# Cross attention over 8192 keys: maxima of the scores from the keys' high parts on two row groups, single score banks, denominators shared out anew

## The reference, cut to what matters

```python
s = q_h @ k_h.T * scale          # 512 x 8192; layer 0 masks keys by mask[q, key]
p = exp(s - max(s, axis=-1))     # softmax over the keys
out_h = (p @ v_h) / p.sum(axis=-1)
x = x + concat(out_h) @ Wo.T + bo
```

## Time and profile before

| | us |
|---|---|
| median of 3 runs | 4553.37 (4545.86 to 4557.13) |
| the profiled execution, its own time | 4563.42 |
| its span (first to last instruction) | 4561.7 |
| cross attention of layer 0, of the span | about 400 to 1595 |
| cross attention of layer 1, of the span | about 2660 to 3730 |
| TensorE busy in the whole span | 4016.3 (88%) |
| VectorE, ScalarE, GpSimd busy | 3028.8, 2097.2, 2085.6 |

### The profile page before, as it was taken

The page is one execution under the profiler, slowest core; times in us unless marked ns, Lnnn a source line. Parts: engine busy times, 40 slices in busy tenths (PEclk is TensorE's granted clock), DMA queues, the critical chain, the costliest instruction groups (busy, mean ns, idle before and its releaser), DMA issues. The chain is left out here.

```text
span 4561.7 us, 51244 instructions
## 1 busy us (share of the span) xinstructions
PE 4016.3 (88%) x17552; PEld 2239.1 (49%) x17552; DVE 3028.8 (66%) x5006; ACT 2097.2 (46%) x2331; POOL 2085.6 (46%) x1224
## 2 busy tenths in 40 slices
PE   7996999999999866669999869999999969769997
PEld 6883344444444242127777634444444425347775
DVE  3334777777777159954777658787877634477776
ACT  2220354555545424322666516555555621347665
POOL 0001698998989715510000029988898940000000
PEclk9996899999999877988999969999999978789998
DMA  8998566665666410011788748988888850308886
GB/s 304 329 335 276 133 143 142 145 142 139 147 133 146 91 42 9 0 66 43 279 300 302 259 133 205 210 205 199 199 201 191 185 125 1 103 30 308 301 304 230
DMA packets 301553, 802.04 MB, mean 176 GB/s; under 512 B 55793, under 2 KB 89329, under 8 KB 263920
## 3 DMA queue, kind: packets, MB, share of 16 engines
q1 hardware_dynamic: 231312, 560.19, 36.3%
q0 software_dynamic: 61280, 221.80, 23.7%
q10 hardware_dynamic: 8704, 16.78, 1.1%
HBM read 484.23 MB, written 98.37 MB: 128 GB/s over the span
## 5 line engine op out<-in xcount | busy, mean ns | idle before, releaser
L855 POOL TENSOR_TENSOR den_pool<-den_pool,prob 128x1024 f32<-128x1024 f32 x444 | 1162.9, 2619 | 54.1 <-ACT prob L696 35.0
L696 ACT ACTIVATE prob<-psum 128x1024 f32<-128x1024 f32 x752 | 768.4, 1024 | 623.7 <-PE psum L610 599.7
L588 PE MATMUL psum<-k_ring,q_stack 98*128 98x512 f32 x2048 | 905.1, 465 | 120.9 <-DVE row_max L746 43.5
L610 PE MATMUL psum<-q_stack,k_ring 98*128 98x512 f32 x2048 | 870.1, 496 | 2.3 <-ACT prob L696 1.3
L746 DVE CUSTOM_DVE_ANT_0 psum<-psum,mask_q 128x512 f32<-128x512 f32 x1024 | 702.5, 706 | 255.0 <-PE psum L588 253.2
L742 DVE TENSOR_REDUCE row_max<-psum 128x1 f32<-128x512 f32 x1024 | 681.5, 688 | 214.5 <-PE psum L588 210.8
L588 PEld LDWEIGHTS psum<-k_ring,q_stack 98*128 98x128 f32 x2048 | 402.6, 197 | 808.9 <-issue 473.0
L1811 DVE TENSOR_TENSOR weight_lo<-weight_raw,weight_hi 128x2048 fp32r<-128x2048 f32 x240 | 547.1, 2289 | 163.0 <-ACT weight_hi L1754 162.8
L1754 ACT ACTIVATE weight_hi<-weight_raw 128x2048 fp32r<-128x2048 f32 x240 | 454.3, 1915 | 42.3 <-DMA weight_raw<-in_L_ffn_w 23.1
L855 POOL TENSOR_TENSOR den_pool<-den_pool,xnT 128x1024 f32<-128x1024 f32 x164 | 419.8, 2560 | 20.4 <-ACT xnT L696 11.3
L610 PEld LDWEIGHTS psum<-q_stack,k_ring 98*128 98x128 f32 x2048 | 405.3, 199 | 45.4 <-ACT prob L696 16.0
(11 more groups left out here) (415 smaller groups left out, 6277.5 us busy)
## 6 DMA issues: line engine op xcount, KB each, us to landing
den_dma<-prob POOLq DMA_DIRECT2D x260, 512.0 KB, 5.2
weight_raw<-in_L_ffn_w SPq DMA_DIRECT2D x120, 1024.0 KB, 6.7
k_ring<-k_hi SPq DMA_DIRECT2D x1024, 64.0 KB, 2.5
weight_raw<-in_L_ffn_Wu SPq DMA_DIRECT2D x60, 1024.0 KB, 7.0
weight_raw<-in_L_ffn_Wd SPq DMA_DIRECT2D x60, 1024.0 KB, 4.9
den_dma<-xnT POOLq DMA_DIRECT2D x92, 512.0 KB, 5.1
k_ring<-k_lo SPq DMA_DIRECT2D x512, 64.0 KB, 3.0
den_pool<-den_dma POOLq DMA_DIRECT2D x48, 512.0 KB, 5.4
```

What stands on the lines that cost most here:

```text
L588: e.matmul(k.bank(maxbank[i % 2]), q_stack[h % n_q][:, i * P:(i + 1) * P], k_ring[:, n % kring, :], start=True, stop=True).then_inc(s_max, 1)
L610: ins = e.matmul(k.bank(kt), k_ring[:, n % kring, kt * P:(kt + 1) * P], q_stack[h % n_q][:], start=not masked, stop=True)
L696: e.activation(prob[g % n_p], k.psum[:, 2 * j2:2 * j2 + 2, :], ACT.Exp, scale=scale).then_inc(s_exp, 1)
L855: e.tensor_tensor(den[:], den[:], tile, ALU.add).then_inc(s_dpool, 1)
```

## The change

- **Maxima from the high parts.** The maximum matmuls use 32 rows, q high against k high. Two matmuls make one step: rows 0 to 31 with one chunk of keys, rows 32 to 63 with the next chunk (both groups of rows of `k_ring` hold the high part; `q_stack` now gets the high part three times, and its low part is loaded by `load_q_lo` after the maxima of the head are through). A step fills two banks (2 and 3, or 4 and 5), and VectorE reduces 1024 columns at once. A head has 32 steps, one for each pair. The step stands between the scores of the pair's two blocks. The maxima run LEAD = 3 steps beyond one head ahead, `top_of_rows` moves from pair 30 to pair 28. The rows of the maximum need not be zero during the maxima, so `zero_rows` is gone.
- **Single score banks.** A block's score fills bank 0 or bank 1, and ScalarE takes exponentials of 512 columns, 64 a head.
- **Denominators.** Layer 0: VectorE adds tiles 0 to 4 (four additions of 128 x 1024 at pairs 3 to 6), GpSimd 18, DMA 9 as before. Layer 1: TensorE sums 11 tiles (pairs 0, 3, ..., 30): a wave has three blocks of values and a fourth matmul of 32 columns of ones, in the fourth column group, so a head has 22 waves; DMA takes 7 tiles with one accumulator and one merge, GpSimd 14 (13 additions).
- **Division in pieces.** The reciprocal and the product of four heads are cut into four pieces of 128 columns each, at pairs 16 to 23.
- Buffers: `prob` has 7 tiles in layer 0 (6 before), `k_ring` 22 and 36 chunks (20 and 32 before), the values come in quarters, and the output weights have a place of their own.

```diff
-LEAD = 1
+LEAD = 3
...
+class Waves:
+
+
+    def __init__(self, by_pe):
+        self.cols = 3 if by_pe else 4
+        self.count = -(-KT // self.cols)
+        self.by_pe = by_pe
+
+    def blocks(self, w):
+        return range(self.cols * w, min(self.cols * (w + 1), KT))
+
+    def sum_block(self, w):
+
+        return 6 * (w // 2) + w % 2
...
+    def step(self, w):
+
+        return -(-(self.cols * (w + 1)) // 2)
...
-    n_q, n_p = 3, 6 if masked else 10
-    kring = NKC + LEAD + (3 if masked else 15)
+    n_q, n_p = 3, 7 if masked else 10
+    kring = 22 if masked else 36
+    if masked:
+        sums = Sums([0, 1, 2, 3, 4], [], list(range(5, PAIRS - 2, 3)))
+    else:
+        sums = Sums([], list(range(0, PAIRS, 3)), [7, 10, 14, 17, 20, 25, 28])
+    waves = Waves(sums.by_pe)
...
-    sums = Sums(range(5, PAIRS - 2, 3), 1) if masked else Sums(range(5, PAIRS - 2, 2), 2)
...
+        return k.psum[:, 2 + 2 * (q % 2):4 + 2 * (q % 2), :].rearrange("p b n -> p (b n)")
...
-                for g, part in enumerate((0, 1, 0)):
-                    e.dma_start(q_stack[h % n_q][g * DH:(g + 1) * DH, :].bitcast(F32), q_hi_lo[part][rows, :]
+                    e.wait_ge(s_score, KT * (h - n_q + 1))
+                for g in range(3):
+                    e.dma_start(q_stack[h % n_q][g * DH:(g + 1) * DH, :].bitcast(F32), q_hi_lo[0][rows, :]
                                 ).then_inc(s_q[h % n_q], 16)
+
+            def load_q_lo(h):
+                e.wait_ge(s_max, PAIRS * (h + 1))
+                e.dma_start(q_stack[h % n_q][DH:2 * DH, :].bitcast(F32), q_hi_lo[1][h * DH:(h + 1) * DH, :]
+                            ).then_inc(s_q[h % n_q], 16)
...
+                if c == LAST_SUM // 2 and h + 1 < H:
+                    load_q_lo(h + 1)
...
+            def maxima(q):
+                h, r = divmod(q, PAIRS)
+                c2, i = divmod(r, TT)
+                n = NKC * h + 2 * c2
+                if r == 0:
+                    e.wait_ge(s_q[h % n_q], 64 * (h // n_q) + 48)
                 if i == 0:
-                    if c == 0:
-                        e.wait_ge(s_q[h % n_q], 48 * (h // n_q + 1))
-                    if c == 0 and h >= n_q:
-                        e.wait_ge(s_zero, h - n_q + 1)
-                    if n < kring:
-                        e.wait_ge(s_ring, n_q + n + 1)
                     e.wait_ge(s_k[n % kring], 48 * (n // kring + 1))
-                if 4 * n + i >= 2:
-                    e.wait_ge(s_red, 4 * n + i - 1)
-
-                e.matmul(k.bank(maxbank[i % 2]), q_stack[h % n_q][:, i * P:(i + 1) * P], k_ring[:, n % kring, :],
-                         start=True, stop=True).then_inc(s_max, 1)
+                    e.wait_ge(s_k[(n + 1) % kring], 48 * ((n + 1) // kring + 1))
+                if q >= 2:
+                    e.wait_ge(s_red, q - 1)
+                for a in range(2):
+                    rows = slice(a * DH, (a + 1) * DH)
+                    ins = e.matmul(max_banks(q)[:, a * KC:(a + 1) * KC], q_stack[h % n_q][rows, i * P:(i + 1) * P],
+                                   k_ring[rows, (n + a) % kring, :], start=True, stop=True)
+                ins.then_inc(s_max, 1)
...
-            def scores(g):
-                h, p = divmod(g, PAIRS)
-                n, j2 = divmod(g, 2)
-                if p == 0:
+            def scores(b):
+                h, t = divmod(b, KT)
+                n, kt = divmod(b, 4)
+                if t == 0:
                     e.wait_ge(s_mlo, h + 1)
-                if g >= 2:
-                    e.wait_ge(s_exp, g - 1)
-                for j in range(2):
-                    kt = 2 * j2 + j
-                    if masked:
-                        e.matmul(k.bank(kt), k.ident_big[:], masks[1][:, 2 * p + j, :], start=True, stop=False)
-                    ins = e.matmul(k.bank(kt), k_ring[:, n % kring, kt * P:(kt + 1) * P], q_stack[h % n_q][:],
-                                   start=not masked, stop=True)
-                ins.then_inc(s_score, 1)
+                    e.wait_ge(s_q[h % n_q], 64 * (h // n_q + 1))
+                if b == 0:
+                    e.wait_ge(s_ring, kring)
+                if b >= 2:
+                    e.wait_ge(s_exp, b - 1)
+                if masked:
+                    e.matmul(k.bank(b % 2), k.ident_big[:], masks[1][:, t, :], start=True, stop=False)
+                e.matmul(k.bank(b % 2), k_ring[:, n % kring, kt * P:(kt + 1) * P], q_stack[h % n_q][:],
+                         start=not masked, stop=True).then_inc(s_score, 1)
...
+                if waves.by_pe:
+                    t = waves.sum_block(w)
+                    ins = e.matmul(vbank[3 * DH:4 * DH, :], k.ones[:, 0:DH],
+                                   prob[(PAIRS * h + t // 2) % n_p][:, t % 2, :], start=w == 0,
+                                   stop=w == waves.count - 1, skip_group_check=True)
...
+                scores(2 * g)
+                if g + PAIRS + LEAD < H * PAIRS:
+                    maxima(g + PAIRS + LEAD)
+                scores(2 * g + 1)
+                waves_after(h, p)
...
+            def exponentials(b):
+                e.wait_ge(s_score, b + 1)
+                if b % 2 == 0:
+                    tile_free(b // 2)
+                e.activation(prob[b // 2 % n_p][:, b % 2, :], k.bank(b % 2), ACT.Exp, scale=scale).then_inc(s_exp, 1)
...
-                    e.reduce_max(out, bank, AXIS_X).then_inc(s_red, 1)
+                    e.reduce_max(out, max_banks(q), AXIS_X).then_inc(s_red, 1)
...
-                e.tensor_tensor_reduce(out=bank, in0=bank, in1=masks[0][:, i, chunk_cols(c)], scale=1.0,
+                    e.wait_ge(s_maskq, 4 * c2 + 2 + i // 2 + 1)
+                e.tensor_tensor_reduce(out=max_banks(q), in0=max_banks(q),
+                                       in1=masks[0][:, i, 2 * c2 * KC:2 * (c2 + 1) * KC], scale=1.0,
...
-            def zero_rows(h):
-                e.wait_ge(s_score, reused_stack(h))
-                e.memset(q_stack[h % n_q][rows_m, :].bitcast(F32), 0.0).then_inc(s_zero, 1)
+            def add_tile(h, j):
+
+                p = sums.by_dve[j + 1]
+                den, tile = den_pool[h % 2], prob[(PAIRS * h + p) % n_p]
+                e.wait_ge(s_exp, 2 * (PAIRS * h + p) + 2)
+                if j == 0:
+                    if h >= 2:
+                        e.wait_ge(s_head, h - 1)
+                    e.tensor_tensor(den[:], prob[PAIRS * h % n_p], tile, ALU.add).then_inc(s_ddve, 1)
+                else:
+                    e.wait_ge(s_ddve, sums.dve_adds * h + j)
+                    e.tensor_tensor(den[:], den[:], tile, ALU.add).then_inc(s_ddve, 1)
...
+            def divide(g, n, cols):
+                e.wait_ge(s_rec, n)
+                e.tensor_tensor(attT[:, g, cols], attT[:, g, cols], den4[:, cols], ALU.mult).then_inc(s_rec, 1)
...
+                if p == LAST_SUM and h + 1 < H:
                     top_of_rows(h + 1)
...
+                if 3 <= p < 3 + sums.dve_adds:
+                    add_tile(h, p - 3)
...
+                if 16 <= p < 24 and h % 4 == 0 and h > 0:
+                    done, cols = 8 * (h // 4 - 1) + p - 16, slice((p - 16) // 2 * P, ((p - 16) // 2 + 1) * P)
+                    (divide if p % 2 else reciprocal)(h // 4 - 1, done, cols)
...
-            def merge(h, a):
...
+            def merge(h):
 
                 e.wait_ge(s_dpool, sums.pool_adds * (h + 1))
-                e.wait_ge(s_ddma[a], 16 * sums.acc_adds[a] * (h + 1))
-                if a > 0:
-                    e.wait_ge(s_merge, 16 * (sums.n_acc * h + a))
-                e.dma_start(den_pool[h % 2][:], den_dma[a][:], accum_op=ALU.add).then_inc(s_merge, 16)
+                e.wait_ge(s_ddma, 16 * len(sums.by_dma) * (h + 1))
+                e.dma_start(den_pool[h % 2][:], den_dma[:], accum_op=ALU.add).then_inc(s_merge, 16)
```

330 lines of the change are left out of this document (168 added, 162 removed).

## The result

The changed kernel takes 5249.65 us (median of 4 runs, 5240.10 to 5263.05) against 4555.25 (4545.86 to 4566.56) before: ratio 1.1525, 95% interval 1.1486 to 1.1564, slower by 15%. That is far outside my range of 4350 to 4710.

A forecast was written before the change was run, and what follows sets the result against it. TensorE bounds layer 0; TensorE and VectorE hold each other up in layer 1. Layer 0 +17 - 18 = -1, layer 1 +74 + 4 - 20 = +58, together +57: 4620 profiled, 4610 median; range 4350 to 4710 (8 in 10).

The forecast's parts named there:

- the clock at 0.97 or above: Expected TensorE clock; its rival, chance 0.06: gaps at steps put a tenth of both stages at 1.2 GHz, 4810 us.
- The step of two 32-row matmuls: Maxima on TensorE: side by side, 0.555 us in layer 0 and 0.665 in layer 1, against 0.47 before.
- The free change of division: Rival at the maxima step: changing the array's division costs nothing for row groups, step 0.265, about 4360 us; chance 0.14.
- the serial matmuls: Rival at the maxima step: its two matmuls run one after the other, +0.2 us on 960 steps, 4800 us; chance 0.08.
- Cycles: TensorE's cycle of two pairs: 4.08 us in layer 0 against 4.02, and 3.94 in layer 1 against 3.41 measured before.
- Heads: Cross attention time per head: 67.6 us in layer 0, none of 74, and 65.4 in layer 1 against 60.5.
- Openings: Starts of the cross attentions, bound by mask loads and reductions: no change, within 10 us either way.
- Division in pieces: Reciprocal and product on VectorE: -18 us from layer 0's long heads, +4 us in layer 1.
- Six further waves: Layer 1's added waves on TensorE: 6 x 1.215 = 7.3 us a head, the matmul of ones free.
- The tail: Layer 1's end, 72.2 us before: 39 for TensorE and 11 for last addition, merge and landing; taken as -20 us.
- SyncE's late low part: `load_q_lo` goes out at about pair 29, 6 us before the next head's scores need it: no cost.
- Additions that collide, late exponentials: Rivals: VectorE's additions wait on GpSimd's, 4670 us; ScalarE's exponentials, at worst 30 us. Chance of either 0.14.

The follow-up runs named there:

- e13: e2 with one more matmul of 32 rows and 8 columns ahead of each maxima step; 4997 us, ratio to before 1.099.
- e2: Changed kernel with both maximum matmuls of a step over all 96 rows, low part in the stack from the start; 4619 us, ratio to before 1.0147.
- e11: Changed kernel with both maximum matmuls over the same 64 rows, without the product with the keys' low part; 5582 us, ratio to before 1.2228.
- e14: Changed kernel with each step's two 32-row maximum matmuls issued twice into the same banks; 5603 us, ratio to before 1.2328.
- e3: Changed kernel with the next head's maxima rows turned one pair earlier, in pair 29 instead of 30; 4831 us, ratio to before 1.0647.
- e12: Changed kernel with every score matmul of layer 1 issued twice into the same bank; 4990 us, ratio to before 1.0978.
- e6: Changed kernel with both maximum matmuls of a step on the same 32 rows, one row group; 5659 us, ratio to before 1.2422.
- e7: Kernel before with only the division cut into eight pieces over pairs 16 to 23; 4533 us, ratio to before 0.9959.
- e4: Changed kernel with 96-row maxima and layer 0's shares in layer 1 (16 waves a head, no sums on TensorE); 4573 us, ratio to before 1.0057.
- e9: e3 with the copies of a finished head moved one pair later, to pair 13; 4733 us, ratio to before 1.0309.
- e8: Changed kernel with 32-row maxima kept, 16 waves a head in layer 1 and the turn in pair 29; 5018 us, ratio to before 1.1002.
- e5: Changed kernel with 96-row maxima, 16 waves a head in both layers and the turn in pair 29; 4521 us, ratio to before 0.9927.

## Why the prediction was wrong

The step that failed is the clock: "the clock at 0.97 or above". I had it as a rival with 0.06, a tenth of both stages at 1.2 GHz and 4810 us, and gave it the wrong cause: gaps "in which nothing streams". By the earlier trace rows such gaps had done no harm in the kernel before, so I held the clock for safe. e13 shows that this half was right: with a bare load on every step the clock stays at 0.95. What keeps it low is what streams: matmuls of 512 columns over 32 rows, two to a step, where 98-row matmuls had been (e2 and e13 against e11 and e14). In its place the runs showed 0.58 in layer 1, which is 607 of the 680 us in its 15 heads. None of the rows that I had read holds more than 2 us of such matmuls, but the trace of the kernel before does: 38 us over 32 and 64 rows, busy throughout, at 0.50 (1695 to 1733 us, above). I hadn't read it when I gave the clock 0.06.

The Trainium skill (TensorE: Matmul & The Clock Gate, "Why this matters for your kernels") wants long idle gaps kept out of TensorE's work if the clock is to stay. This case differs: in layer 1 TensorE was busy 685 of 700 us at 0.58, and the waits behind which the clock fell lasted 0.6 to 2.1 us; the measurement decides.

Layer 0 has the same steps and kept 0.95, and 1.00 with the early turn (e3). It has a mask's matmul of 128 rows with every score, so four full ones to a step where layer 1 has two. That fits e12, which gave layer 1 four by doubling its scores (0.92); no run took the masks out of layer 0, so for that layer it is argued and not shown. A second thing is not shown. The step over 64 rows has a bare load ahead of it, like the one over 32 (0.34 us in e11), and the step over 96 rows has none, so the array's division changes between 64 and 96 rows too. Whether the rows or the division keep the clock low while the step streams, no run here separates; that 64 rows hold layer 0 better than 32 speaks for the rows.

Point by point, the rest of the sum:

- **The step of two 32-row matmuls.** Forecast 0.555 in layer 0 and 0.665 in layer 1, measured 0.51 and 0.615. Right in mechanism and within 0.05: side by side, and dearer than two full ones (0.47). The free change of division and the serial matmuls fell as rivals; e6 shows what the latter cost. The Trainium skill's rule that a change of tiling mode drains TensorE (TensorEngine Tiling (Array Packing), Key Properties) agrees with the bare loads.
- **Cycles.** Forecast 4.08 and 3.94; measured 3.97 in layer 0, from one wave's start to the next (1200.37 to 1204.34), and 3.84 in layer 1 at the full clock.
- **Heads.** Forecast 67.6 and 65.4. With the early turn (e3) they are 66.0 and, where the clock held, 66.3: right. In the changed kernel layer 0's were mostly 69.3 to 70.0, with four of 72.5 and more. The term that I left out is the turn, which I took over at 2.3 and 2.4 us: the maxima's rows come in pair 30 and the new head's first score waits 1.6 us for them, 15 times in layer 0 (23 us in all), and 10 of the 13 waits between 600 and 1500 us are followed by 3 to 20 us at the low clock. e3 gives 14 of layer 0's heads 51 us back.
- **Layer 1 at the full clock.** No run has the changed kernel at the full clock. e2 took 4619 us, and its steps in layer 1 are 0.10 us cheaper; 4619 + 480 x 0.10 is about 4670, an estimate. With the clock given, the sum of 4610 would have come out some 60 us low, and the waits at 30 turns (1.6 to 1.7 us each, 50 us) are most of that.
- **Openings.** Forecast nothing, within 10. From layer 0's last copy to layer 1's first it is 54.6 us more, at a clock of 0.50 from 2696 to 2867 us; in e2 that stretch is 3.6 us more. So this too is the clock.
- **Division in pieces.** Forecast -18 in layer 0 and +4 in layer 1; e7 has -21 in all, but by its heads 10 us come from layer 0 and 14 from layer 1. The sum is near by luck, and the mechanism in layer 0 gave half of what I put. In the changed kernel itself long heads stayed, since the clock's dips took their place.
- **Six further waves.** Forecast 7.3 x 15 = 110 us within layer 1's +74 net; e4 against e2 has 46. Where the sums don't run on TensorE, other waits (reductions, 33 us in e4) take part of the gain.
- **The tail.** Forecast -20 on the 72.2 us from the last copy but one to `head_out`. Measured it is 62.5 (4327.6 to 4390.1), 10 us less: TensorE took 52 us for the last head where I put 39, and the rest, put at 11, took 10.4 without a wait for the merge. That the stretch behind the last copy became 20.4 us shorter is another stretch, and luck.
- **SyncE's late low part.** I said nothing would come of it. It arrives up to 2.1 us after the score that needs it wants to start (e2, e9). In the changed kernel the wait for the maxima's rows hid it, but for one of 1.8 us.
- **Additions that collide, late exponentials.** No sign: VectorE's additions took 1.22 us each, as priced, GpSimd's got faster (median 2.37 us against 2.54 in the earlier trace rows), and matmuls wait for an exponential only once or twice a head, behind the copies of the finished head (10 us in all of layer 0). In layer 1 that wait of 0.63 us is cheap as time, but the clock falls behind it.

Shown: that maxima over few rows hold layer 1 at the low clock, that it is their columns and not the bare loads, that neither side-by-side running nor the added waves is the cause. Every fall in layer 1 of e3, e9 and, from 2860 to 3620 us, of the changed kernel stands behind a wait of 0.5 to 2.1 us; not every such wait brings a fall. Open: in which heads the clock comes back, and so why e8 is worse than e3, where between 64 and 96 rows the change lies in layer 1, and whether it is the rows or the division of the array.

## What to carry to other kernels

Read the granted clock beside TensorE's busy time before counting columns. Look through the whole trace of the kernel before for a stretch with the shapes that the change brings, whatever stage it is in. A matmul that uses few rows saves no time by itself (a step of two over 32 rows took 0.51 and 0.62 us, two full ones 0.47) and may cost the clock of everything around it; layer 1's heads took 103 us instead of 66 that way, and adding full matmuls made it faster. Where such matmuls can't be avoided, look for waits as short as one microsecond at the seams of the loop, since the clock falls behind them. Here the version to keep is e5: full-depth maxima over two chunks, single banks, division in pieces, sums off TensorE and the turn a pair earlier, 4521 us. Of its 32 us under the kernel before, the division in pieces alone has 21 (e7, same session).
